# First step's x loaded and normalised inside the scan, and five idle products of TensorE ahead of the feed-forward stage's first transposes

## The reference, cut to what matters

```python
def _layernorm(x, axis=-1, eps=1e-05):
    m = jnp.mean(x, axis=axis, keepdims=True)
    v = jnp.var(x, axis=axis, keepdims=True)
    return (x - m) / jnp.sqrt(v + eps)
...
        residual = x
        xn = layernorm(residual, ln_w, ln_b)
        y = mamba2_mixer(xn, in_proj_w, conv_w, conv_b, dt_bias, A_log, D_skip, rms_w, out_proj_w)
        out = y + residual
        h = layernorm(out, ln_w, ln_b)
        h = jax.nn.relu(h @ mlp_w1 + mlp_b1) @ mlp_w2 + mlp_b2
        return h + out
...
    x = x + _layernorm(_L0_attn_ref(_layernorm(x, axis=-1), ...), axis=-1)
    x = x + _layernorm(_L0_ffn_ref(_layernorm(x, axis=-1), ...), axis=-1)
```

## Time and profile before

| what | value |
|---|---|
| time, median of 3 runs | 954.77 us (954.52 to 955.15) |
| the profiled execution | 954.1 us, of which the span from the first to the last instruction is 952.4 |
| TensorE | 702.2 us busy (74%) |
| VectorE | 640.4 us busy (67%) |
| ScalarE | 484.3 us busy (51%) |
| GpSimd | 464.0 us busy (49%) |
| mean granted clock of TensorE | 0.835 of full speed |

### The profile page before, as it was taken

How to read it: one execution, slowest core, us unless ns; L and a number is a source line. 1 busy time by engine, 2 the same in 40 slices (tenths; PEclk the granted TensorE clock), 3 DMA queues, 4 the chain that set the end, 5 groups by cost and what they waited for, 6 DMA issues and landing times. The chain is left out here.

```text
span 952.4 us, 15550 instructions
## 1 busy us (share of the span) xinstructions
PE 702.2 (74%) x4187; PEld 559.7 (59%) x4187; DVE 640.4 (67%) x2281; ACT 484.3 (51%) x1243; POOL 464.0 (49%) x590
## 2 busy tenths in 40 slices
PE   7457999999999993999898334275677867787600
PEld 3225777777777762989898224243566756676500
DVE  7656999999999954799898576793223222322387
ACT  4754566676666654878685224162222222222356
POOL 7502666676666762243333500004666666666462
PEclk8876999999999995999999555556978889888955
DMA  8920000000000006000000075003122212221197
GB/s 216 365 88 1 1 1 1 2 1 1 2 1 1 1 2 177 1 2 2 2 0 2 0 113 67 0 0 79 45 67 65 68 44 66 64 69 42 45 304 216
DMA packets 73233, 52.96 MB, mean 56 GB/s; under 512 B 11744, under 2 KB 67048, under 8 KB 72896
## 3 DMA queue, kind: packets, MB, share of 16 engines
q1 hardware_dynamic: 67312, 41.61, 16.5%
q0 software_dynamic: 5120, 10.37, 4.2%
q10 hardware_dynamic: 720, 0.05, 0.1%
HBM read 28.04 MB, written 24.18 MB: 55 GB/s over the span
## 5 line engine op out<-in xcount | busy, mean ns | idle before, releaser
L817 DVE SCALAR_TENSOR_TENSOR s_cv<-s_pU,tap_w,s_cv 128x256 f32<-128x256 f32 x384 | 159.6, 477 | 20.0 <-ACT s_cv L761 19.6
L1834 ACT ACTIVATE e_h<-e_pH,e_b 128x256 f32<-128x256 f32 x160 | 65.3, 472 | 166.7 <-remote 105.7
L1776 POOL DMA_INDIRECT e_xg<-token_rows,token_of x80 | 82.0, 1025 | 127.6 <-issue 127.6
L1810 PE MATMUL e_pH<-e_xgT,e_w 128*128 128x256 f32 x320 | 93.3, 443 | 51.2 <-issue 50.5
L1783 POOL DMA_INDIRECT choice_rows<-e_yo,choice_of x80 | 80.5, 1006 | 63.0 <-DVE e_yo L1879 39.6
L1810 PEld LDWEIGHTS e_pH<-e_xgT,e_w 128*128 128x128 f32 x320 | 67.3, 221 | 65.5 <-issue 54.8
L1820 PE MATMUL e_pO<-e_w,e_h 128*128 128x128 f32 x640 | 87.1, 287 | 6.1 <-issue 5.4
L1820 PEld LDWEIGHTS e_pO<-e_w,e_h 128*128 128x128 f32 x640 | 81.7, 204 | 8.9 <-issue 8.9
L637 POOL TENSOR_TENSOR s_xa<-s_xt,arena 128x512 f32<-128x512 f32 x32 | 34.4, 1075 | 103.2 <-ACT s_xt L779 103.2
L1872 DVE TENSOR_TENSOR e_ysum<-e_pO,e_b 128x256 f32<-128x256 f32 x40 | 17.0, 425 | 95.3 <-PE e_pO L1820 44.7
L666 PE MATMUL s_pU<-arena,w_in 128*128 128x262 f32 x256 | 72.3, 407 | 11.7 <-DVE s_cv L817 8.4
(11 more groups left out here) (285 smaller groups left out, 1862.8 us busy)
## 6 DMA issues: line engine op xcount, KB each, us to landing
choice_rows<-zrow SPq DMA_DIRECT2D x16, 512.0 KB, 7.2
arena<-choice_rows SPq DMA_DIRECT2D x32, 256.0 KB, 5.1
token_rows<-arena SPq DMA_DIRECT2D x8, 520.0 KB, 12.6
n_x<-in_L_attn_x_dram SPq DMA_DIRECT2D x8, 512.0 KB, 7.6
arena<-in_L_attn_x_dram SPq DMA_DIRECT2D x8, 512.0 KB, 4.6
e_w<-in_L_ffn_W_dram SPq DMA_DIRECT2D x16, 256.0 KB
out_dram<-arena SPq DMA_DIRECT2D x16, 256.0 KB, 4.4
decay_rows<-arena SPq DMA_DIRECT2D x2, 1024.0 KB, 4.7
```

The lines of the kernel that those rows point to most:

```text
L817: v.scalar_tensor_tensor(out=by_tile(cv[:, p % 2, m, :]), in0=columns(m)[:, :, tap:tap + P], scalar=tap_w[:, m, tap:tap + 1], in1=by_tile( ...
L1776: g.indirect_dma_start(xg[:, n % RING, i, :], None, table, bass.IndirectOffsetOnAxis(ap=token_of[:, G * n + i:G * n + i + 1], axis=0), bou ...
L1810: ins = pe.matmul(pH[n % 2][half_][:, ROWS * c:ROWS * (c + 1)], we1[:, expert(n), P * f:P * (f + 1)], xgT[:, n % 2, :], start=True, stop=True)
L1834: ins = a.activation(hb[:, n % 2, f, :], pH[n % 2][half_][:, ROWS * c:ROWS * (c + 1)], ACT.Silu, bias=be1[:, expert(n), f:f + 1])
```

## The change

It has two parts. The first takes the work for groups 0 to 3 of the feed-forward stage ahead into the scan: SyncE loads x of step 0 (tiles 0 to 7) into an array of its own, `x_first`, at the scan's start; GpSimd makes `mr` and `minus_m` there; and ScalarE writes `res` for the four groups from `x_first`, two instructions after `silu_z` of each of the scan's last four pairs. In the feed-forward stage `centre_x` returns at once for groups 0 to 3, and neither ScalarE's list nor VectorE's waits for x or for `minus_m` at its start. SyncE's own loads into `rows` stay as they were. The second part puts five products of zeros ahead of TensorE's list in the feed-forward stage, into `pM1`, which is not read before `down` has overwritten it.

```diff
+        FRONT = 4
+        x_first = sb("x_first", [P, SEQS, D])
+        res = sb("m_res", [P, FRONT, 2, D])
+        minus_m, mr = sb("minus_m", [P, TILES]), sb("mean_rstd", [P, TILES])
...
             @block.sync
             def _(sp):
 
-                sp.sem_inc(carrier[0], 1)
+                sp.dma_start(x_first[:, :, :], x.rearrange("b (s p) d -> s p b d", p=P)[0]).then_inc(s_xf, 16)
...
                     g.tensor_tensor(yg[:, p % 2, :], y2[:, :], zs[:, p % 2, :], ALU.mult).then_inc(s_yg, 1)
+                g.tensor_tensor(mr[:, :], mean[:, :], rstd[:, :], ALU.mult).then_inc(s_mr, 1)
+                g.wait_ge(s_mr, 1)
+                g.tensor_scalar(minus_m[:, :], mr[:, :], -1.0, None, ALU.mult).then_inc(s_mm, 1)
                 g.wait_ge(s_z0, 1)
                 staged([(1, carry_a), (1, scale), (3, gated), (1, skip)])
...
+                def residual_first(p):
+
+                    q = p - PAIRS + FRONT
+                    if q < 0:
+                        return
+                    if q == 0:
+                        a.wait_ge(s_xf, 16)
+                        a.wait_ge(s_mm, 1)
+                    for i in range(2):
+                        t = 2 * q + i
+                        a.activation(res[:, q, i, :], x_first[:, t, :], ACT.Identity, bias=minus_m[:, t:t + 1], scale=rstd[:, t:t + 1])
                 staged([(0, first_tap(0)), (0, first_tap(1)), (1, silu_b), (1, silu_c), (5, projected), (1, silu_x), (0, first_tap(2)),
-                        (0, first_tap(3)), (1, silu_bt), (4, turned), (4, squares), (2, silu_z)])
+                        (0, first_tap(3)), (1, silu_bt), (4, turned), (4, squares), (2, silu_z), (2, residual_first)])
...
-                g_.tensor_tensor(mr[:, :], mean[:, :], rstd[:, :], ALU.mult).then_inc(s_extra, 1)
-                g_.wait_ge(s_extra, 1)
-                g_.tensor_scalar(minus_m[:, :], mr[:, :], -1.0, None, ALU.mult).then_inc(s_r, 1)
                 skewed8(g_, [(0, residual_bias), (8, add_x), (11, keep)])
...
                 def centre_x(g, m):
 
+                    if isinstance(g, int) and g < FRONT:
+                        return
                     a.wait_ge(s_x[m // 4], 16 * (g // 8 + 1) if isinstance(g, int) else 16 * ((g - m) >> 3) + 16)
...
-                a.wait_ge(s_r, 2)
                 skewed8(a, [(0, centre_x), (1, root(0)), (7, root(1)), (10, root(2)), (3, turned), (12, turned_xl), (4, relus)])
...
                 def residual(g, m):
                     k = m % NB
-                    need(v, s_res, g)
+                    need(v, s_res, g, FRONT)
...
                 v.reciprocal(root_y[:, :], sd_y[:, :]).then_inc(s_r, 1)
-                v.wait_ge(s_r, 2)
+                v.wait_ge(s_r, 1)
...
             @block.tensor
             def _(pe):
+                for _ in range(5):
+                    pe.matmul(pM1[:, :], ones[:, :], zrow[:, 0:512], start=True, stop=True)
+
                 def turn(g, m):
```

More of the change, by code:

```diff
@@ L592, in build @@
             s_far, s_ext, s_inv, s_all, s_row = (sem("s_" + n) for n in ("far", "ext", "inv", "all", "row"))
+            s_xf, s_mr, s_mm = (sem("s_" + n) for n in ("xfirst", "mr", "mm"))
             block = st.enter_context(nc.Block())
@@ L1071, in pst @@
                 return st.enter_context(nc.psum_tensor(name, shape, F32))
-            root_y, sd_y, minus_m, mr = (sbt("m_" + n, [P, TILES]) for n in ("rooty", "sdy", "mm", "mr"))
-            res = sbt("m_res", [P, NB, G, D])
+            root_y, sd_y = (sbt("m_" + n, [P, TILES]) for n in ("rooty", "sdy"))
             h0 = sbt("m_h0", [P, NB, G, D])
@@ L1091, in build @@
             (s_r, s_res, s_h0, s_h0b, s_pT, s_hT, s_ph, s_h1a, s_h1b, s_pm, s_at, s_un, s_x1, s_xl, s_keep, s_px, s_xlT, s_pl,
-             s_lg, s_hn, s_extra) = (sem("m_" + n) for n in (
+             s_lg, s_hn) = (sem("m_" + n) for n in (
                  "r", "res", "h0", "h0b", "pT", "hT", "ph", "h1a", "h1b", "pm", "at", "un", "xone", "xl", "keep", "px",
-                 "xlT", "pl", "lg", "hn", "extra"))
+                 "xlT", "pl", "lg", "hn"))
             s_ph2 = sem("m_ph2")
```

## The result

The changed kernel takes 942.79 us (median of four runs, 941.98 to 943.21) against 954.77 before (median of three; one further execution of that kernel took 3254.91 us and is left out); the ratio is 0.9873 (95% interval 0.9854 to 0.9892). The forecast was 948.1, with a range from 946.2: the direction was right, and 5.3 us of gain were not foreseen. Its profiled execution took 943.2 us, 10.9 less than the 954.1 of the one before, and the spans differ by as much.

A forecast was written before the change was run, and what follows sets the result against it. At the feed-forward stage's start VectorE waited for ScalarE's `res` and TensorE ran the first two groups at half clock. An earlier start (2.6 us) plus the clock (4.1) make 6.7: 954.77 to 948.1 us, range 946.2 to 952.4.

The forecast's parts named there:

- x and `res` ahead: Feed-forward start: VectorE's first `residual` no longer waits for ScalarE and starts at 363.35, 2.92 us earlier.
- The scan's cost: Scan's end: four inserted ScalarE pairs of 0.8 us mostly fall into holes; 0.3 us taken, bounds nothing to 3.3.
- Five products: TensorE at feed-forward start: they take 6.4 us, end at 367.8, hidden before transposes at 368.3; bounds 4.5 to 8.8.
- signs of being wrong: Transposes waiting for products, `up` of group 0 at 3.8 us, taps over half a microsecond late, or gain lost by stage's end.
- The path at full clock: Feed-forward start on TensorE: `up` of groups 0, 1, 2 at 369.3, 372.9, 376.6; 6.7 us earlier taken.
- B: Feed-forward start: clock not up for the first products, only the earlier start's 2.6 us left; 952.2 us, chance 0.15.
- C: Clock falls once more between `turn` and `up` of group 1, TensorE losing 1.7 us; 949.9 us, chance 0.18.
- The split into "start" and "clock": Feed-forward start: of the 6.7 us gain, 2.6 come from the earlier start and 4.1 from the clock.
- Nothing in the stage after that hangs on a fixed time: Feed-forward stage after `up` of group 2: the gain carries through, SyncE's loads staying ahead of readers even 7 us earlier.
- rival E: Feed-forward loop: the clock's fall at 470 to 474 doesn't recur, 1.6 us more gain; 946.5 us, chance 0.06.
- rival G: Experts' stage: five short clock falls become long, costing TensorE 8.5 us in all; 956.6 us, slower, chance 0.05.

The follow-up runs named there:

- x_only: Changed kernel without its five products, only the first x moved into the scan; 950.64 us, ratio to before 0.9937.
- a_pre100: Changed kernel with 100 empty semaphore increments on VectorE at the scan's end, loop at 1358 to 1702; 951.89 us, ratio to before 0.9959.
- a_body: Changed kernel with one more empty semaphore increment in each of eight groups of VectorE's loop body, 353 instructions again; 951.76 us, ratio to before 0.9955.
- w_only: Kernel before with the five products and nothing else; 954.53 us, ratio to before 0.9963.
- w_eight: Kernel before with eight products ahead of the transposes and nothing else; 951.83 us, ratio to before 0.9960.
- a_pre9: Changed kernel with nine empty semaphore increments on VectorE at the scan's end, loop at 1267 to 1611; 950.52 us, ratio to before 0.9934.
- b_pre100: Kernel before with 100 empty semaphore increments on VectorE at the scan's end, loop at 1359 to 1711; 957.63 us, ratio to before 1.0015.
- b_body: Kernel before with the first four `res` marks on their own semaphore, shortening VectorE's loop to 345 instructions; 951.51 us, ratio to before 0.9965.
- a_pre160: Changed kernel with 160 empty semaphore increments on VectorE at the scan's end, loop at 1418 to 1762; 957.93 us, ratio to before 1.0035.
- prod4: Changed kernel with four products in place of five; 948.63 us, ratio to before 0.9909.

## Why the prediction was wrong

**x and `res` ahead: right.** Expected was a first `residual` 0.07 us behind `root_y`, 2.92 earlier. It came at 363.08, 0.04 behind the 363.04 at which `root_y` ended. x_only alone has 2.9 us.

**The scan's cost: 0.3 us taken, about nothing measured.** Timelines of the changed kernel near the scan's end, for the earlier trace rows, ScalarE and VectorE:

```profile
330.09 0.87 ACT L825 ACTIVATE m_res<-x_first,minus_m,rstd 128x128 f32<-128x128 f32 x2
330.86 1.01 ACT L769 ACTIVATE s_cv<-s_pU,tap_b,tap_w 128x256 f32<-128x256 f32 x2
```

```profile
326.69 2.51 DVE L836 SCALAR_TENSOR_TENSOR s_cv<-s_pU,tap_w,s_cv 128x256 f32<-128x256 f32 x6 [0.43 <-ACT s_cv L769]
...
331.45 2.51 DVE L836 SCALAR_TENSOR_TENSOR s_cv<-s_pU,tap_w,s_cv 128x256 f32<-128x256 f32 x6 [0.20 <-ACT s_cv L769]
...
335.14 1.72 DVE L836 SCALAR_TENSOR_TENSOR s_cv<-s_pU,tap_w,s_cv 128x256 f32<-128x256 f32 x4 [0.26 <-ACT s_cv L769]
```

The taps of the round before ran 0.26 us ahead of the old kernel's (326.69 for 326.95), and those of pair 31 0.08 ahead (331.45 for 331.53): the insertion cost 0.18 us there. But the next taps are 0.25 ahead again (335.14 for 335.39), since VectorE's next wait shrank from 0.43 to 0.26. What I had not looked at is the wait behind the one I costed; it was large enough to swallow it.

**Five products: 6.4 us taken, 7.50 measured, and not hidden.** They began at 361.06 and ended at 368.56; `hn` was complete at 367.71, and the transposes began at 368.40, some 0.6 us late. The 6.4 had taken over the slow beginning of the first stage; how many products run slow depends on when the clock rises, and the five took 5.96 (a_pre100) to 7.58 us (a_body). This is a mis-sized term inside its own bounds of 4.5 to 8.8, and one of the prediction's own signs of being wrong, that the first transposes wait for the products, came true. That they began at 368.40 for the 368.3 forecast is in part luck: `hn` was there 0.5 us sooner than summed, since the scan cost nothing and the stage began 0.24 us earlier, and the products took that back.

**The path at full clock: right.** `up` of groups 0 and 1 at 369.3 and 372.9 forecast, 369.44 and 373.13 measured; group 2 at 376.6 and 376.94, which is 6.56 us earlier than the earlier trace rows for the 6.7 taken. Neither B nor C came about; the clock stayed at 1.00 from 367 on. The rule of the Trainium skill ("TensorE: Matmul & The Clock Gate", Part 4) that transposes don't count as busy for the clock did not cost anything here: the transposes took 0.38 us, where they took 0.69 at 0.50 before, and the clock stayed at 1.00 behind them. So they do run at the full clock. Whether they would raise or hold it by themselves this run can't say, with products on both sides. The split into "start" and "clock" stands with one addition, by w_only and w_eight: the clock's 3.4 to 4.0 us need products that end close before the transposes, and five do that only because x is ahead.

**The step that failed** is "Nothing in the stage after that hangs on a fixed time". From `up` of group 2 the stage gained another 4.3 us: 3.2 at the back edge (7.59 for 4.38) and 1.2 where the clock no longer fell (5.59 for 4.37). I had seen the fall in the earlier trace rows and gave it, as rival E, 1.6 us and 6%, with the phase of the engines as its cause. I had not seen the stall in front of it, and not asked what the new argument in VectorE's wait does to the program. E's place was right; its cause was not, and the larger part of what happened, 3.2 of 4.4 us, was outside it. One sum is off as well, with nothing hanging on it: half of the difference between 6.8 and 3.6 us is 1.6 and not 1.7, so rival G's 8.5 is 8.0 and its time 956.1.

**How firm the cause is.** Shown: the stall comes and goes with the place of VectorE's loop in its program alone (a_pre9 against the changed kernel, b_pre100 against before), and at one place with its length alone (b_body against before, a_body against the changed kernel), and with it come five more code packets in each execution. Argued: that the loop must lie within three blocks of 128 instructions. Three packets on q14, 8 KB each, fall into the 15 us around each of the six stalls, where a smooth back edge has none or one. The Trainium skill, page "Runtime: NRT & Kernel Launch", section "Instruction fetch mechanics", describes such a stall at a taken branch whose target is no longer loaded; it gives blocks of 16 KiB, or 256 instructions, two of which are held. By that section's size of an instruction a packet of 8 KB would hold 128 of them, an estimate that fits the blocks the runs suggest. The runs agree with the stall, and not with the size of the blocks: by that rule the loop at 1418 to 1762 fits into two blocks with edges near 1350, 1606 and 1862, and it stalled. The fall of the clock followed four of the six stalls (not w_eight, not a_pre160) and no execution without one; what decides it stays open.

## What to carry to other kernels

Where a hardware loop shows an "issue" wait of microseconds at its back edge, count the loop's instructions and their place in that engine's program: one register computation less per round, or a shift of the whole, can take the stall away, and a shift by nine instructions can bring it back. Before costing an edit, compare the instruction counts of every engine's loops, since even one argument of a wait changes them. Products that warm the clock pay only when they last until it has risen (two did not) and end close ahead of the work they are for; look at the idle time between the last of them and that work, and at the waits that follow an inserted piece, which may swallow it.

## What the runs showed of the hardware

A loop of 345 or 353 instructions ran its back edge in no extra time at some places of VectorE's program and lost 1.9 to 3.1 us at others, with packets of 8 KB on q14; the eight places tried fit blocks of 128 instructions. Where it ran smoothly, its second pass needed no packet on that queue (448 to 488 in the changed kernel). TensorE's clock, once at 1.00, was still there after idle gaps of 1.15 us (w_eight) and 1.54 us (prod4), and was down to 0.50 by the first `up` behind one of 3.51 us (w_only). The same five products took between 5.96 and 7.58 us. Transposes of one pair took 0.38 us at 1.00 and 0.69 at 0.50. An empty semaphore increment is not free: 100 of them at the end of the scan put `root_y` back by 3.6 us (362.49 to 366.07), and 60 more lengthened VectorE's idle time there by another 5.57 us (8.96 to 14.53), 0.09 us each.
